# A fused feed-forward / state-space / feed-forward kernel: how its layer norms get the inverse deviation to all partitions

## The reference

```python
x = x + 0.5 * ffn(layernorm(x));  x = x + ssm(layernorm(x));  x = x + 0.5 * ffn(layernorm(x))

layernorm(x) = (x - mean(x)) / sqrt(var(x) + 1e-5)      # over the 512 channels
ffn(x)       = (sigmoid(x @ Q(w1).T) * (x @ Q(w2).T)) @ Q(w3).T    # hidden 1408, Q(w) = clip(round(w/mean|w|), -1, 1)
ssm(x):  xz = x @ W_x.T;  dt = softplus(xz[:128] @ W_dt.T + b_dt);  B, C = xz[128:144], xz[144:160]
         h[t] = exp(dt * -exp(A_log)) * h[t-1] + dt * B * x;   y = sum_n h * C + x * D     # 16 states per channel
```

## Time and profile before

| | us |
|---|---|
| median of 3 runs (787.21 to 796.45) | 792.58 |
| the profiled execution | 794.82 |
| span of its profile | 793.0 |
| busy: PE / DVE / ACT / POOL | 636.6 / 640.2 / 569.3 / 644.4 |
| mean granted TensorE clock, share of full | 0.914 |

### The profile page before, as it was taken

How to read it: one execution, slowest core, us unless ns; L and a number is a source line. 1 busy time by engine, 2 the same in 40 slices (tenths; PEclk the granted TensorE clock), 3 DMA queues, 4 the chain that set the end, 5 groups by cost and what they waited for, 6 DMA issues and landing times.

```text
span 793.0 us, 14028 instructions
## 1 busy us (share of the span) xinstructions
PE 636.6 (80%) x4872; PEld 523.8 (66%) x4872; DVE 640.2 (81%) x825; ACT 569.3 (72%) x1344; POOL 644.4 (81%) x523
## 2 busy tenths in 40 slices
PE   4798775397889987997889987988889888348898
PEld 4577653286668765876667765876667766236787
DVE  3863898899877998699878997798959997599831
ACT  5864756878786879587886879678877779377441
POOL 0181999999988999699988999799988989689812
PEclk8699997599989999899999999999989999659999
DMA  9501678887748878497748777588829766968100
GB/s 355 167 1 44 155 173 177 213 185 180 160 103 186 167 169 188 89 215 180 166 98 196 162 161 186 138 172 183 199 57 211 160 139 161 208 154 167 28 27 27
DMA packets 42438, 121.06 MB, mean 153 GB/s; under 512 B 5888, under 2 KB 14848, under 8 KB 42368
## 3 DMA queue, kind: packets, MB, share of 16 engines
q0 software_dynamic: 18864, 68.69, 46.5%
q1 hardware_dynamic: 23504, 51.49, 19.5%
HBM read 47.03 MB, written 4.46 MB: 65 GB/s over the span
## 4 chain that ended last, share of the span: by engine, by line
PE 30%; ACT 19%; POOL 16%; DVE 16%; issue 15%; DMA 3%; DVEq 1%; ACTq 0%; POOLq 0%
PE work L413 22%; DVE states L988 9%; POOL shared L1201 8%; PE stat L413 6%; ACT decay L767 6%; POOL shared L1214 3%; DVE shared L1001 3%; ACT shared L787 2%; ACT tanh L720 2%; DMA shared<-shared 2%; POOL square L308 2%; ACT hid_hi L728 2%; POOL hid_lo L1181 1%; ACT dt L753 1%; DVE hid L953 1%
## 5 line engine op out<-in xcount | busy, mean ns | idle before, releaser
L413 PE MATMUL work<-x_hi,q 128*128 128x256 f16 x1408 | 333.8, 284 | 39.3 <-DVE hid L953 21.3
L1201 POOL TENSOR_TENSOR shared<-u,b_row 128x1024 f32<-128x1024 f32 x127 | 345.2, 2720 | 0.5
L413 PE MATMUL work<-x_lo,q 128*128 128x256 f16 x1408 | 333.1, 284 | 0.0
L767 ACT ACTIVATE decay<-dt,a_neg 128x256 f32<-128x256 f32 (+1 forms) x512 | 220.7, 464 | 102.1 <-DVE states L988 101.4
L988 DVE TENSOR_TENSOR_SCAN states<-decay,last_state,shared 128x512 f32<-128x512 f32 x224 | 279.8, 1277 | 9.3 <-ACT shared L787 3.5
L1181 POOL TENSOR_TENSOR hid_lo<-hid,hid_hi 128x256 f16<-128x256 f32 x176 | 147.8, 1082 | 96.2 <-ACT hid_hi L728 96.0
L413 PEld LDWEIGHTS work<-x_hi,q 128*128 128x128 f16 x1408 | 143.7, 102 | 75.8 <-DVE hid L953 33.9
L413 PE MATMUL work<-hid_hi,q 128*128 128x256 f16 x693 | 159.2, 279 | 8.3 <-POOL hid_lo L1181 6.1
L1001 DVE TENSOR_TENSOR shared<-states,c_row 128x1024 f32<-128x1024 f32 x128 | 155.7, 1217 | 7.8
L413 PE MATMUL work<-hid_lo,q 128*128 128x256 f16 x693 | 158.7, 278 | 0.0
L413 PEld LDWEIGHTS work<-x_lo,q 128*128 128x128 f16 x1408 | 143.3, 102 | 22.0
(11 more groups left out here) (118 smaller groups left out, 665.1 us busy)
## 6 DMA issues: line engine op xcount, KB each, us to landing
shared<-shared POOLq DMA_DIRECT2D x131, 512.0 KB, 5.3
b_row<-bc_dram SPq DMA_DIRECT2D x32, 512.0 KB, 5.8
c_row<-bc_dram SPq DMA_DIRECT2D x32, 512.0 KB, 6.2
x_in<-xT SPq DMA_DIRECT2D x8, 512.0 KB, 7.0
outT<-shared SPq DMA_DIRECT2D x7, 512.0 KB, 5.5
shared<-w1T SPq DMA_DIRECT2D x4, 704.0 KB, 8.5
shared<-w2T SPq DMA_DIRECT2D x4, 704.0 KB, 12.1
shared<-w3T SPq DMA_DIRECT2D x3, 768.0 KB, 13.4
```

The lines of the kernel that those rows point to most:

```text
L413: return nc.tensor.matmul(out, lhsT, rhs, start=start, stop=stop)
L767: ins = nc.scalar.activation(decay[pair][:, j, j:TC], dt[:, par, k, j:TC], ACT.Exp, scale=a_neg[:, k, n:n + 1])
L1201: nc.gpsimd.tensor_tensor(dbx[:, g % DBX_RING, :, :], u[:, par, :, :], bcast(b_row[:, group % 2, n % ROWS, :]), ALU.mult).then_inc(dbx_don ...
```

## The change

PE now puts the variance on all partitions at once: `mean_w` is the stationary side and the squares, all four channel tiles, are the moving side. ACT then computes exp(-0.5 * ln(var + eps)) on the whole 128 x 256 tile, in two instructions with `log_var` between them, and writes it to the place in the bank from which `normalise` reads. So `fold_squares` on POOL, `invert_std` and `half_invert` on DVE, `ln_spread_of` and `half_spread_of` on PE, the identity matrix, the copy into `first_spread` and their semaphores go. The places of the four tables are new throughout.

```diff
 AT_PE = dict(
-    down1=[123, 130, 131, 133], ... mean0=152, ... mean1=140, ... mean2=123, ... spread0=153, ... spread1=143,
-    ... spread2=132, ... up2=[140, 140, 142, 143, 150, 151, 152, 152, 152, 152, 153], ... var0=153, var1=142, var2=131
+    down1=[123, 123, 140, 140], ... mean0=152, ... mean1=141, ... mean2=110, ...
+    up2=[142, 143, 143, 150, 151, 152, 152, 152, 152, 152, 152], ... var0=153, var1=143, var2=132
 AT_ACT = dict(
-    ... gate2=[81, 92, 110, 110, 120, 121, 130, 140, 140, 141, 142],
-    hi2=[112, 112, 112, 112, 130, 131, 131, 141, 141, 142, 142], square0=130, square1=81, square2=60,
-    std0=141, std1=90, std2=61, x_hi0=151
+    ... gate2=[100, 101, 102, 120, 120, 130, 130, 131, 140, 141, 142],
+    hi2=[101, 122, 130, 131, 131, 132, 132, 141, 141, 142, 142], spread0=150, spread1=91, spread2=62,
+    square0=132, square1=90, square2=60, x_hi0=150
 AT_DVE = dict(
-    ... hid2=[90, 110, 112, 120, 130, 131, 132, 141, 142, 143, 150], norm0=151, norm1=93, norm2=71, recip0=142, ...
+    ... hid2=[102, 110, 120, 130, 130, 132, 132, 133, 142, 142, 142], norm0=150, norm1=100, norm2=72, ...
 AT_POOL = dict(
-    add_y=31, add_y_last=11, fold_sq0=141, fold_sq1=82, fold_sq2=51, fold_x0=92, ... u=132, x_lo0=152, x_lo2=80
+    add_y=12, add_y_last=11, fold_x0=121, ... u=132, x_lo0=151, x_lo2=81
...
             def half_var_of(i, n, j):
...
-                    ins = mm(half_bank(i, j)[:, 1, 0:1], square[i][:, k, token_half(j)], mean_w[:, 0:1], k == 0, k == KD - 1)
+                    ins = mm(half_bank(i, j)[:, 1, 0:P], mean_w[:, :], square[i][:, k, token_half(j)], k == 0, k == KD - 1)
...
+            def ln_var_of(i, count, bank=stat):
+
+                pe.wait_ge(ln_square[i], count)
+                for k in range(KD):
+                    ins = mm(bank[:, 1, :], mean_w[:, :], square[i][:, k, :], k == 0, k == KD - 1)
                 ins.then_inc(ln_var[i], 1)
...
+            def inverse_deviation(i, var, part, out, logged, count):
+
+                n = 0 if i == 1 else 1
+                nc.scalar.activation(part, var, ACT.Ln, scale=1.0 if i == 1 else 1.0 / (X_SCALE * X_SCALE),
+                                     bias=zero_eps[:, n:n + 1]).then_inc(logged, 1)
+                act.wait_ge(logged, count)
+                return nc.scalar.activation(out, part, ACT.Exp, scale=-0.5)
+
+            def half_spread_of(i, n, j, out):
                 act.wait_ge(half_var, n + j + 1)
...
+                inverse_deviation(i, half_bank(i, j)[:, 1, 0:P], log_var[:, token_half(j)], out, half_log, n + j + 1).then_inc(half_spread, 1)
+
+            def ln_spread_of(i, count, bank=stat):
 
                 act.wait_ge(ln_var[i], count)
...
+                inverse_deviation(i, bank[:, 1, :], log_var[:, :], bank[:, 1, :], ln_log[i], count).then_inc(ln_spread[i], 1)
...
-            for j in range(2):
-                act.wait_ge(half_spread, j + 1)
-                nc.scalar.activation(first_spread[:, token_half(j)], half_bank(1, j)[:, 1, 0:P], ACT.Copy).then_inc(first_spread_copied, 1)
...
-            def fold_squares(i, count):
-                pool.wait_ge(ln_square[i], count)
-                fold(pool, nc.gpsimd, fold_sq[i], count, square[i], square[i])
```

More of the change, by code:

```diff
@@ L72 @@
-AT_POOL = dict(
[L73 to L78, removed]
+    down1=[123, 123, 140, 140], down1_first=[132, 132, 140, 140], down2=[153, 153, 153, 153],
@@ L152, in macaron @@
         square = [sb(f"square{i}", [P, KD, TC]) for i in range(3)]
-        std = [sb(f"std{i}", [P, TC // P]) for i in range(3)]
-        rstd = [sb(f"rstd{i}", [P, TC // P]) for i in range(3)]
+        log_var = sb("log_var", [P, TC])
         x_hi = sb("x_hi", [P, 2, KD, TC], F16)
@@ L200, in macaron @@
         ln_var = [sem(f"ln{i}_var") for i in range(3)]
-        ln_std = [sem(f"ln{i}_std") for i in range(3)]
-        ln_rstd = [sem(f"ln{i}_rstd") for i in range(3)]
+        ln_log = [sem(f"ln{i}_log") for i in range(3)]
         ln_spread = [sem(f"ln{i}_spread") for i in range(3)]
@@ L558, in _ @@
                 ffn_down(0, 0, m)
-            ln_var_of(0, 2, True, decay[0])
+            ln_var_of(0, 2, decay[0])
             ffn_down(0, 0, 2)
-            ln_spread_of(0, 2, decay[0])
             ffn_down(0, 0, 3)
@@ L597, in beside_scan @@
                     if now == at(AT_PE, c, "var2"):
[L598 to L600 removed]
+                        ln_var_of(2, c)
                 if not last(c):
@@ L838, in _ @@
             ln_square_of(0, 2)
-            ln_std_of(0, 2, decay[0])
+            ln_spread_of(0, 2, decay[0])
             ln_hi_of(0, 2, 0)
@@ L933, in centre @@
                 nc.vector.tensor_tensor(centred[i][:, :, :], src, bcast(bank[:, 0, :]), ALU.subtract).then_inc(ln_centred[i], 1)
-            def invert_std(i, count):
-                dve.wait_ge(ln_std[i], count)
-                nc.vector.reciprocal(rstd[i][:, :], std[i][:, :]).then_inc(ln_rstd[i], 1)
             def normalise(i, count, out, bank=stat):
@@ L1078, in _ @@
                 half_centre(1, j, x2(0))
-            for j in range(2):
-                half_invert(1, 0, j)
             dve.wait_ge(bc_mm, 1)
-            dve.wait_ge(first_spread_copied, 2)
+            dve.wait_ge(half_spread, 2)
             nc.vector.tensor_tensor(bc_out[:, :], states[0:BC, 0, :], first_spread[0:BC, :], ALU.mult).then_inc(bc_read, 1)
             for j in range(2):
-                half_normalise(1, 0, j, xln)
+                half_normalise(1, 0, j, xln, first_spread[:, token_half(j)])
             dve.wait_ge(dt_raw_mm, 1)
@@ L1154, in _ @@
             for j in range(2):
-                half_invert(2, 2, j)
-            for j in range(2):
-                half_normalise(2, 2, j, centred[2])
+                half_normalise(2, 2, j, centred[2], half_bank(2, j)[:, 1, 0:P])
             for j in range(2):
```

143 lines of the change are left out of this document (41 added, 102 removed).

## The result

The changed kernel takes 815.0 us in the median of four runs (814.1 to 817.2) against 794.0 for the kernel before beside it: ratio 1.028, 95% interval 1.023 to 1.033. The forecast was 770, with a range to 797. One execution of 2050 us, of the kernel before with `add_y` at 12, was in a slow state and is left out of its median.

The account below looks back on a forecast made before the run. Waits between nearly equally busy POOL, DVE and PE were taken to bound it, mostly at the chunk boundary. POOL -3.5, boundary -27, opening +3.2 and ending +4.2 sum to -23: 794.8 to 771.7, median 770, range 754 to 797.

Parts of the forecast that it names:

- I cost it at nothing: POOL's queue: `add_y` moving from place 31 to 12 costs nothing, covered by the removed folds; without that cover, 16 us.
- ACT gains 0.6 us per norm, hidden under its 101 us of waits: ACT at each norm: Ln, load, Exp add 0.6 us, hidden under 101 us of waits for DVE.
- rival C: ACT's block starves the scan: scans wait for decays behind a norm, giving 814 us; chance 0.13.
- The boundary, -27: Chunk boundary at norm 0: second residual done 4.5 us earlier (bounds 1.0 and 6.6) in six chunks, -27 us.
- Opening, +3.2: Opening: first norm +1.3, norm of chunk 1 +0.6, chunk 0's halves +1.3; sum +3.2 us (1 to 6).
- Ending, +4.2: Ending: PE starts at 763.3, not 760.10, +3.2; low clock after PE stands idle, +1.0; sum +4.2 us (2 to 6).
- Loads: ACT's table loads: Ln and Exp each need one, 69 in place of 62, five more in opening, two in ending.
- rival A: ACT: one table serves Ln and Exp, with no load between them; 62 loads and 761 us; chance 0.12.
- POOL, -3.5: Mid-chunk on POOL: 21 folds of squares removed, counted as 0.5 us per period, seven times, -3.5 us.
- the main case: Whole kernel: the summed terms give 770 us, own range 762 to 780; chance 0.52.

Follow-up runs that it names:

- The moved transfers: Store and c_row load issued some 3.5 us later: changed kernel 801.4 us; with one activation, 773.0 (`add_y` at 12) and 772.0 (`add_y` at 31).
- one activation: Changed kernel with Abs_reciprocal_sqrt in place of Ln, load, Exp: 773.9 us with `add_y` at 31, 787.1 with `add_y` at 12.
- the version with no load at all in the block: Changed kernel, `add_y` at 12, with Exp in the place of Ln, so no norm needs a table load: 765.0 us, ratio 0.964.
- the grouping of the halves: Changed kernel, `add_y` at 31, with opening's norm 1 and ending's norm halves as Ln, Ln, Exp, Exp (65 loads): 794.9 us.
- `add_y` at 31: Changed kernel with `add_y` of chunks 1 to 6 put back from 12 to 31: 799.7 us, ratio 1.007.
- without loads in norm 0: Changed kernel, `add_y` at 12, with Exp in the place of Ln in norm 0 of chunks 3 to 7 alone: 798.9 us, ratio 1.006.

## Why the prediction was wrong

**The failed step: "I cost it at nothing".** The move of `add_y` was covered, the prediction said, by the folds that are gone; without the cover it would be 6 x 2.6 = 16. It cost 15.3. That the bound fits is luck: there were five long waits of 5.1 to 6.6 us, each of which cost 2.1 to 3.1 us in step 4. The folds' time is there (POOL is busy 75 us a period instead of 81), but it doesn't help the product: POOL waits 2.82 us for `x_hi`, and `x_hi` for ACT's block. The prediction had the block ending at 232.4 and PE's end of it worked out, and never followed `x_hi` and `x_lo` to POOL's queue, where the last products stand behind them. Nor did it see that the product, once it comes with or behind the store and the `c_row` load, lands 4 to 5 us later. The moved transfers show it: with POOL equally late the cost is gone.

**"ACT gains 0.6 us per norm, hidden under its 101 us of waits".** The sum for ACT's busy time was about right, and beside the point: what grew is the time from variance to factor. Before, the first load ran ahead of the variance and the second behind the root, beside DVE and PE, as ACT's rows of the kernel before at norm 1 show (start, us, instruction):

```profile
285.30 1.28 ACT L705 ACT_TABLE_LOAD   x1
287.71 0.26 ACT L705 ACTIVATE std<-stat,zero_eps 128x2 f32<-128x2 f32 x1 [1.13 <-PE stat L413]
287.99 1.28 ACT L767 ACT_TABLE_LOAD   x1
```

A load between Ln and Exp can't be hidden so. At norm 0 it was counted (2.7, measured 2.77). At norms 1 and 2 it was not. At norm 1 DVE waits 2.42 in every chunk from 1 to 6, where it waited 0 to 1.6 before, and step 9 grows by 9.0 in sum; at norm 2 it waits 0.8 at most. With one activation step 9 is at -1.3. ACT's waits for DVE fell from 101 to 62 us, but this is not rival C. DVE waits for the norm's own factor; the decays behind it are there in time (done at 303.5, the scan starts at 303.86 without a wait), and over the whole span scans wait for decays 1.2 us in two waits, against 1.1 in three before. C hit its number by luck.

**The boundary, -27.** Right in its parts: no idle PE, clock 1.00 in the block, a stall of 2.77. Chunks 1 to 5 gain 4.0, 3.7, 2.4, 2.8 and 4.0 us in their last two steps, for a forecast of 4.5; but chunk 0, counted as a sixth, loses 3.5. It had no wait at its norm 0 to lose; now DVE stands 2.56 there for ACT's Exp and 0.81 for a decay. The sum is -13.4, so this term was 13.6 short.

**Opening, +3.2; measured +7.0.** The halves end at 75.4 and `bc_out` starts 2.95 later than before, where 3.2 was the whole sum. Two things came on top. PE, idle 3.84 us for it, then ran the z block at clock 0.55: 3.61 us for eight matmuls that took 1.99 before, at clock 1.00 behind 2.03 us of idling. And the first `hidden` now stands ahead of the first scan: from the first decay to the scan it is 3.94 us (83.33 to 87.27) instead of 1.40. The prediction priced nothing for gates that move by a few places; with one activation the same 3.94 is there (77.19 to 81.13), and is made up for by an earlier start.

**Ending, +4.2; measured +4.6.** From the last square to PE's start 8.76 us (772.36 to 781.12) against 5.50: 3.26, for a forecast of 3.2.

**Loads.** 69 as forecast, so rival A, one load for both, is out. The Trainium skill, "ScalarE: Activation LUTs", section "Table sets: the hidden batching unit", has exp and ln in one set, so that ln and then exp cost one load. The trace disagrees: it has a load ahead of each of 26 Ln and each of 26 Exp. By that rule the block would be one load, 2.1 us; the version with no load at all in the block bounds what that could give at 50 us, the wait at `add_y` among them, the grouping of the halves shows 4.8 for four loads. Section "What ACT_TABLE_LOAD costs" adds a drain to each switch; the load at 240.86 starts where `hid_hi` ends (240.84) and Ln 0.01 behind the load, so there is none.

**POOL, -3.5.** The steps other than 4, 9, 14 and 15 changed by 0.0 in sum, -1.5 with `add_y` at 31. Small, as said, and smaller.

**The range** left out C with 0.13. Between the forecast's -23.1 and the ledger's +22.4 lie 45.5 us: boundary 13.6, `add_y` 12.8, norm 1 9.0, opening 3.8, POOL 3.5, last chunk 2.5 (forecast at nothing, and not followed up), ending 0.4. With `add_y` at its own bound (+16) and norm 1 at DVE's stall, the main case would have been 770 + 16 + 9 = 795, just inside the range to 797.

## What to carry to other kernels

Count a table load by where it stands, not only by how many there are: here it was hidden ahead of an input or behind a result, and pure delay between the two functions of one chain, and everything that waits for the result gets it, down to another engine's queue. When a step moves, follow the last item ahead of it through every queue to the DMA issues, and ask which other transfers are issued in the same microsecond. A place was free or dear by one microsecond here, so a move that one version bears must be priced again in the next.

## What was not expected of the hardware

DVE's RECIPROCAL took 1756 ns on 128x256 f32 and 936 to 952 on 128x128, against 1220 ns for a product of 128x1024. ACT's Abs_reciprocal_sqrt took 448 ns on 128x256, and had loads of 1283 ns like the others. An accumulating DMA of 512 KB landed 4.8 to 6.1 us after its issue when it was issued a microsecond or more ahead of two transfers of another queue, and 8.8 to 10.4 when it came with them or just behind. Those two took longer in the first case: the store 6.1 to 6.3 us without loads in norm 0, against 3.4 to 4.8 with one activation and `add_y` at 12; in the changed kernel, where the product came 1.2 behind, it took 5.0 to 6.1.
